# Expert outputs of a mixture-of-experts layer: gate weights applied at eviction, and rows added straight into the stored output by serial accumulating scatters

## What is computed

```python
x = x + _L0_ffn_ref(_layernorm(x, axis=-1), wg1, bg1, wg2, bg2, We, be)

h = gelu(xf @ wg1 + bg1, approximate=False)
logits = (h @ wg2 + bg2)[:, :E]                      # E = 20
probs = softmax(logits, axis=-1)
top_vals, top_idx = top_k(probs, K)                  # K = 2
gates = zeros((N, E)).at[arange(N)[:, None], top_idx].set(top_vals)
def body(y, eb):
    We_e, be_e, g_e = eb
    return (y + g_e[:, None] * (xf @ We_e + be_e), None)
```

## Time and profile before

| | |
|---|---|
| median of three runs | 693.65 us |
| the profiled execution | 695.27 us |
| its span, first to last instruction | 693.4 us |
| PE busy | 640.8 us, 92% |
| DVE busy | 443.1 us, 64% |
| ACT busy | 325.6 us, 47% |
| POOL busy | 295.4 us, 43% |
| mean granted TensorE clock | 0.961 of full speed |

### The profile page before, as it was taken

The page is one execution under the profiler, slowest core; times in us unless marked ns, Lnnn a source line. Parts: engine busy times, 40 slices in busy tenths (PEclk is TensorE's granted clock), DMA queues, the critical chain, the costliest instruction groups (busy, mean ns, idle before and its releaser), DMA issues. The chain is left out here.

```text
span 693.4 us, 15963 instructions
## 1 busy us (share of the span) xinstructions
PE 640.8 (92%) x6313; PEld 524.8 (76%) x6313; DVE 443.1 (64%) x1005; ACT 325.6 (47%) x604; POOL 295.4 (43%) x261
## 2 busy tenths in 40 slices
PE   5999999999999999999999979999999856999970
PEld 5668788887888878888788868887788735888850
DVE  4864656666656465575664557444577584999966
ACT  4344444544444344453443235334465422999930
POOL 2205544355434454435543235311244406788520
PEclk9999999999999999999999999999999956999995
DMA  8512465544665436654457530210011855999828
GB/s 329 196 48 50 122 171 124 148 115 125 170 169 119 124 99 170 149 121 125 124 117 182 121 132 16 77 62 2 3 62 62 305 212 193 403 402 360 292 91 323
DMA packets 42967, 107.75 MB, mean 155 GB/s; under 512 B 8180, under 2 KB 8564, under 8 KB 42114
## 3 DMA queue, kind: packets, MB, share of 16 engines
q1 hardware_dynamic: 38482, 98.21, 47.7%
q0 software_dynamic: 4400, 8.41, 3.3%
HBM read 65.61 MB, written 13.44 MB: 114 GB/s over the span
## 5 line engine op out<-in xcount | busy, mean ns | idle before, releaser
L1764 POOL TENSOR_SCALAR pp<-pp,rl 128x400 f32<-128x400 f32 x128 | 164.1, 1300 | 187.9 <-DVE rl L1240 187.8
L865 ACT ACTIVATE pp<-pp,acc 128x400 f32<-128x400 f32 x128 | 79.0, 620 | 66.5 <-DVE acc L1299 66.5
L1299 DVE CUSTOM_DVE_ANT_0 pp<-bank,cap 128x400 f32<-128x400 f32 x128 | 65.9, 571 | 50.9 <-PE bank L362 50.9
L192 PE MATMUL bank<-chi,wk 128*128 128x400 f32 x248 | 87.2, 351 | 0.0
L193 PE MATMUL bank<-clo,wk 128*128 128x400 f32 x248 | 85.5, 345 | 0.0
L194 PE MATMUL bank<-chi,wk 128*128 128x400 f32 x248 | 85.5, 345 | 0.0
L1291 DVE STREAM_TRANSPOSE raw<-pp 128x512 f32<-128x512 f32 x128 | 83.4, 688 | 2.2 <-POOL pp L1764 2.2
L192 PE MATMUL bank<-wv,chi 128*128 128x512 f32 x200 | 82.6, 413 | 0.0
L193 PE MATMUL bank<-wv,chi 128*128 128x512 f32 x200 | 79.3, 396 | 0.0
L194 PE MATMUL bank<-wv,clo 128*128 128x512 f32 x200 | 78.9, 395 | 0.0
L192 PE MATMUL bank<-wh,xu 128*128 128x512 f32 x148 | 62.1, 420 | 0.2 <-DVE xu L1148 0.2
(11 more groups left out here) (252 smaller groups left out, 1304.6 us busy)
## 6 DMA issues: line engine op xcount, KB each, us to landing
pt<-raw SPq DMA_DIRECT2D x256, 128.0 KB, 2.4
wr<-in_We SPq DMA_DIRECT2D x13, 1024.0 KB
craw<-in_ctx SPq DMA_DIRECT2D x15, 800.0 KB, 4.6
raw<-in_We SPq DMA_DIRECT2D x8, 1024.0 KB
acc<-in_We SPq DMA_DIRECT2D x6, 1024.0 KB
scratch_xn<-acc SPq DMA_DIRECT2D x16, 256.0 KB
wr<-scratch_ys SPq DMA_DIRECT2D x8, 512.0 KB, 7.5
x_sb<-in_x SPq DMA_DIRECT2D x2, 1024.0 KB, 12.0
```

The source lines that it names most:

```text
L192: pe.matmul(o, lhs[0], rhs[0], start=start, stop=False)
L865: act.activation(frame(p8), frame(p8), ACT.Exp, bias=bias, scale=-1.0, accum_out=total).then_inc(S["a_exp"], 1)
L1299: dve.tensor_tensor_reduce(out=frame(p8), in0=scores[:, p8 % 4, :], in1=cap[:, :], scale=-1.0, scalar=nm[:, b, p8:p8 + 1] if seg else 3e38 ...
L1764: pool.tensor_scalar(frame(p8), frame(p8), rl[:, n % 2, p8:p8 + 1], None, ALU.mult).then_inc(S["g_pn"], 1)
```

## The change

The gate is applied when a block is evicted, and the evicted rows are added into the output in DRAM.

1. The stream with the biases is stored to the output before the blocks. All eight bias products now stand before the blocks, and SP stores `x_sb` in two DMAs of 1 MB.
2. A table of gates `gtab` (row of the block by block) is made like `tab`: `row_in` times the one-hot of the block scaled by the gate. ScalarE scales (32 instructions), TensorE multiplies (16 matmuls), VectorE adds the high and low parts.
3. The eviction of block n is an activation with the scale `gtab[:, n]`, instead of a plain copy.
4. The scatter of block n goes to the output with `compute_op=ALU.add`. Two experts' blocks can hold the same token, so scatter n waits until scatter n - 1 has landed, and scatter 0 until both stores have.
5. The loading back, the 16 gate-weighted adds and the eight stores at the end are gone; so is `scratch_ys`. With the destination row being the token itself, the normalised rows are stored once, and a second index table `tok2` has the scatter's rows. An empty row 0 of a block is added, with gate 0, to some real row.

```diff
@@ TensorE, before the blocks
+            biases([3])
+            for j in range(16):
+                pe.wait_ge(S["a_gp"], j // 8 + 1)
+                last = pe.matmul(pb[7][:, 0:72], row_in[:, j, :], gate_in[:, j, :], start=(j == 0), stop=(j == 15))
+            last.then_inc(S["p_tab"], 1)
+            biases(range(4, 8))
             turn_tokens(0)
...
-            biases(range(3, 8))
@@ ScalarE, before the blocks
+            act.wait_ge(S["v_gw"], 1)
+            gates = [ghi[:, :, :].bitcast(f32), glo[:, :, :]]
+            for c in range(2):
+                act.wait_ge(S["v_tab"], c + 1)
+                for i in range(8):
+                    for part in range(2):
+                        ins = act.activation(gate_in[:, 8 * c + i, 36 * part:36 * part + BLOCKS], blk_in[:, 8 * c + i, :],
+                                             ACT.Copy, scale=gates[part][:, c, i:i + 1])
+                ins.then_inc(S["a_gp"], 1)
@@ ScalarE, in a block
                 if n >= 4:
                     act.wait_ge(d_yo[n % 4], 16 * (n // 4))
-                copy(yo[n % 4], pb[3 + n % 2][:, :]).then_inc(S["a_y"], 1)
+                elif n == 0:
+                    act.wait_ge(S["v_tok"], 2)
+                act.activation(yo[n % 4], pb[3 + n % 2][:, :], ACT.Copy, scale=gtab[:, n:n + 1]).then_inc(S["a_y"], 1)
@@ VectorE, routing
-            own.on(dve.tensor_tensor(gmg[:, :, :], gmg[:, :, :], sg[:, :].unsqueeze(1).to_broadcast([128, 2, 8]), ALU.mult))
+            chain(dve.tensor_tensor(gmg[:, :, :], gmg[:, :, :], sg[:, :].unsqueeze(1).to_broadcast([128, 2, 8]), ALU.mult))
+            chain(dve.tensor_copy(ghi[:, :, :], gmg[:, :, :]))
+            rest(glo[:, :, :], gmg[:, :, :], ghi[:, :, :]).then_inc(S["v_gw"], 1)
...
+            for i in range(8):
+                dve.wait_ge(S["p_be"], i + 1)
+                dve.tensor_tensor(x_sb[:, i, :], x_sb[:, i, :], pb[(0, 1, 2, 4)[i % 4]][:, :], ALU.add).then_inc(S["v_y"], 1)
+            dve.wait_ge(S["p_tab"], 2)
+            chain(dve.tensor_copy(gtab[:, :], pb[7][:, 0:BLOCKS]))
+            dve.tensor_tensor(gtab[:, :], gtab[:, :], pb[7][:, 36:36 + BLOCKS], ALU.add).then_inc(S["v_tok"], 1)
@@ VectorE, the end
-            biases(range(8))
-            for i in range(8):
-                dve.wait_ge(d_ga[i], 16)
-                for c in range(2):
-                    if c:
-                        dve.wait_ge(S["v_out"], 2 * i + 1)
-                    dve.scalar_tensor_tensor(out=x_sb[:, i, :], in0=yga[:, i, c, :], scalar=gmg[:, c, i:i + 1],
-                                             in1=x_sb[:, i, :], op0=ALU.mult, op1=ALU.add).then_inc(S["v_out"], 1)
@@ POOL, in a block
                 pool.wait_ge(S["a_y"], n + 1)
-                pool.indirect_dma_start(out=t["ys"][:, :],
-                                        out_offset=bass.IndirectOffsetOnAxis(ap=tok[:, n:n + 1], axis=0),
-                                        in_=yo[n % 4], in_offset=None, bounds_check=2 * T + BLOCKS - 1,
-                                        oob_is_err=False).then_inc(d_yo[n % 4], 16)
+                if n:
+                    pool.wait_ge(d_yo[(n - 1) % 4], 16 * ((n - 1) // 4 + 1))
+                else:
+                    pool.wait_ge(S["d_out"], 32)
+                pool.indirect_dma_start(out=out.rearrange("b q d -> (b q) d"),
+                                        out_offset=bass.IndirectOffsetOnAxis(ap=tok2[:, n:n + 1], axis=0),
+                                        in_=yo[n % 4], in_offset=None, bounds_check=T - 1, oob_is_err=False,
+                                        compute_op=ALU.add).then_inc(d_yo[n % 4], 16)
@@ SP, before the blocks
-            for n in (R, 6, 7, R + 1, R + 2):
+            load_weight(R)
+            ov = out.rearrange("(i b) q d -> (b q) i d", b=2)
+            for i in (0, 4):
+                sp.wait_ge(S["v_y"], i + 4)
+                sp.dma_start(ov[:, i:i + 4], x_sb[:, i:i + 4, :]).then_inc(S["d_out"], 16)
+            for n in (6, 7, R + 1, R + 2):
                 load_weight(n)
@@ SP, the end
-            for i in range(8):
-                sp.dma_start(yga[:, i], t["ys"][0:2 * T, :].rearrange("(c i p) n -> i p c n", c=2, i=8)[i]).then_inc(
-                    d_ga[i], 16)
-            for i in range(8):
-                sp.wait_ge(S["v_out"], 2 * i + 2)
-                sp.dma_start(out.rearrange("(i b) q d -> i (b q) d", b=2)[i], x_sb[:, i, :]).then_inc(S["d_out"], 16)
-            sp.wait_ge(S["d_out"], 128)
```

More of the change, by code:

```diff
@@ L130, in perceiver @@
         gmg = sb("gmg", [128, 2, 8])
+        ghi = sb("ghi", [128, 2, 8], f32r)
+        glo = sb("glo", [128, 2, 8])
+        gtab = sb("gtab", [128, BLOCKS])
         warm = sb("warm", [128, 1])
@@ L133, in perceiver @@
         tab = sb("tab", [128, BLOCKS])
-        tok = sb("tok", [128, BLOCKS], u32)
+        tok, tok2 = [sb(f"tok{j}", [128, BLOCKS], u32) for j in range(2)]
         m12 = sb("m12", [128, 2, 8, E])
@@ L148, in perceiver @@
         ji = sb("ji", [1, 16], i32)
-        cs2 = sb("cs2", [128, 576])
+        cs2 = sb("cs2", [128, 612])
         wr = sb("wr", [128, 4, 4, D])
@@ L156, in perceiver @@
         yo = [xm[:, 0, :], xm[:, 1, :], hT[:, 0:D], hT[:, D:T]]
-        yga = wr[:, 0:4].rearrange("p r (a c) n -> p (r a) c n", c=2)
         xflat = [v[:, :, :].rearrange("p k n -> p (k n)") for v in xu]
         row_in = xflat[1][:, 2048:4096].rearrange("p (j r) -> p j r", j=16)
+        gate_in = xflat[1][:, 0:16 * 72].rearrange("p (j b) -> p j b", j=16)
         put_in = [v.rearrange("p k n -> p (k n)")[:, 0:8 * 36].rearrange("p (j b) -> p j b", j=8) for v in g1]
@@ L168, in perceiver @@
         place1, iota, b128 = cs2[:, 360:376], cs2[:, 376:504], cs2[:, 504:504 + BLOCKS]
-        no_place = cs2[:, 539:539 + BLOCKS]
+        no_place, elsewhere = cs2[:, 539:539 + BLOCKS], cs2[:, 574:574 + BLOCKS]
         names = """d_cst d_k1 d_x0 d_x1 d_ctx d_cap d_xn d_raw0 d_raw1 d_par
@@ L177, in perceiver @@
             d_g1 d_gate a_g1 v_g1 p_g1 a_gelu p_lg v_lg a_le v_pre p_cnt v_orep v_tab p_tab v_tok v_ji
-            g_gt v_sg p_gT a_gT p_be v_y g_xi a_we v_we a_wx v_wx p_xo a_xo v_xo p_y a_y v_out d_out
+            g_gt v_sg p_gT a_gT p_be v_y g_xi a_we v_we a_wx v_wx p_xo a_xo v_xo p_y a_y v_gw a_gp d_out
             """.split()
@@ L183, in perceiver @@
         d_yo = [sem(f"d_yo{i}") for i in range(4)]
-        d_ga = [sem(f"d_ga{i}") for i in range(8)]
         d_x = (S["d_x0"], S["d_x1"])
@@ L699, in biases @@
                 for i in which:
-                    if i >= 3:
-                        pe.wait_ge(S["v_y"], i - 2)
+                    if i >= 4:
+                        pe.wait_ge(S["v_y"], i - 3)
                     r = slice(32 * (i % 4), 32 * (i % 4) + E)
-                    pe.matmul(pb[i % 3][:, :], gT[r, i // 4, :], be[r, :], start=True, stop=True).then_inc(S["p_be"], 1)
+                    pe.matmul(pb[(0, 1, 2, 4)[i % 4]][:, :], gT[r, i // 4, :], be[r, :], start=True, stop=True).then_inc(S["p_be"], 1)
             pe.wait_ge(S["g_gt"], 2)
@@ L1658, in vector @@
             chain(dve.tensor_tensor(rb[:, 1, :], slot, rb[:, 0, :], ALU.subtract))
-            dve.wait_ge(S["d_xn"], 272)
+            dve.wait_ge(S["d_xn"], 144)
             for c in range(2):
@@ L1681, in vector @@
             dve.tensor_copy(tok[:, :], tab[:, :]).then_inc(S["v_tok"], 1)
[L1683 to L1686, removed]
+            dve.wait_ge(S["v_tok"], 1)
+            chain(dve.scalar_tensor_tensor(out=tab[:, :], in0=tab[:, :], scalar=float(T), in1=elsewhere, op0=ALU.is_ge,
+                                           op1=ALU.mult))
+            chain(dve.scalar_tensor_tensor(out=tab[:, :], in0=pb[3][:, 0:BLOCKS], scalar=-1.0, in1=tab[:, :],
+                                           op0=ALU.add, op1=ALU.add))
+            own.on(dve.tensor_copy(tok2[:, :], tab[:, :]))
+            for i in range(8):
[4 more added lines that the diff above has]
+            dve.tensor_tensor(gtab[:, :], gtab[:, :], pb[7][:, 36:36 + BLOCKS], ALU.add).then_inc(S["v_tok"], 1)
             def turn_tokens(n):
@@ L1849, in load_tokens @@
                                         in_offset=bass.IndirectOffsetOnAxis(ap=tok[:, n:n + 1], axis=0),
-                                        bounds_check=2 * T + BLOCKS - 1, oob_is_err=False).then_inc(d_xi[n % X], 16)
+                                        bounds_check=T + BLOCKS - 1, oob_is_err=False).then_inc(d_xi[n % X], 16)
             def block_of(n):
@@ L1859, in block_of @@
                 pool.wait_ge(S["a_y"], n + 1)
[L1860 to L1863 removed]
+                if n:
[6 more added lines that the diff above has]
+                                        compute_op=ALU.add).then_inc(d_yo[n % 4], 16)
             pool.wait_ge(S["g_xi"], 1)
[L1866 removed]
+            pool.wait_ge(S["d_xn"], 144)
             pool.wait_ge(S["v_tok"], 1)
@@ L2006, in store_rows @@
                 sp.wait_ge(S["a_nx"], 8 + i + 1)
-                for c in range(2):
```

(17 more changed lines are left out.)

## The result

The changed kernel takes 762.83 us (761.92 to 764.02, four runs) against 693.48 us before: 1.099 times as long, 95% interval 1.097 to 1.1011. Forecast were 730.5 us in a range of 692 to 780. The direction and the mechanism were right. The size was not: 35 us slower were forecast, 69 came.

What follows compares the result with a forecast made beforehand. Bound before: TensorE at 3.19 us a block, POOL and DMA engines about as full. Start 0.5 us, blocks 54.0 and last landing 1.8 more, less 21.0 for the tail: 35.3 us slower, 730.5 us, range 692 to 780.

Steps and rivals of the forecast that it cites:

- the mechanism: Expert blocks: each adding scatter waits for the previous landing; first to last scatter takes 132.8 us instead of 78.8.
- the tail's saving: After the last scatter's landing: reading back, gate-weighted adds and stores go, giving back 21.0 us.
- where the crowd ends: Expert blocks: last weight asked for about scatter 13, so 14 periods at 5.8 us, then 12 at 4.3 us.
- P = L + 0.3: Expert blocks: period from scatter to scatter, or 3.19 us if that is more; 5.8 us crowded, 4.3 us quiet.
- L: Adding scatter, start of issue to landing: 4.0 us quiet, up to 7.9 us in a crowd.
- 2.8 + (2.22 - 0.98): Quiet adding scatter: quickest gather, then the last plain scatter's time without its issue, in series: 4.0 us.
- the end: After the blocks: output complete when the last adding scatter lands, 4.0 us after its issue, at 728.6 us of span.
- the start: Ahead of the blocks: first scatter 0.5 us later, at 591.8 us; VectorE's first tokens 1.8 us later, covered by POOL's gathers.
- rival A: Expert blocks: add hidden, landing under 2.9 us, TensorE keeps 3.19 us a block, tail gone; 676.6 us, chance 0.11.
- B: Rival, expert blocks: mild crowding, quiet 3.5 us landing throughout, period 3.8 us; 696 us, no change, chance 0.08.
- C: Rival, expert blocks: always crowded or add itself slow, landings 6.7 to 7.9 us; 782 to 815 us, chance 0.07.
- D: Rival, expert blocks: TensorE falls to 1.2 GHz, 6.3 us a block; 762 us, chance 0.06 in full.

Runs made afterwards that it cites:

- the free plain version: Changed kernel with plain scatters into four tensors in turn, each waiting only for the fourth before it, full weights: 684.24 us.
- two chains: Changed kernel with even blocks added into the output, odd ones into a second tensor, each scatter waiting for the one before the last: 701.68 us.

## Why the prediction was right or wrong

**Right: the mechanism.** One landing after another sets the pace, and the tail's saving does not pay for it. With four adding scatters in flight instead of one, 66 us are saved (762.8 against 696.9).

**Right: where the crowd ends.** The last weight was asked for at 681.23 us, with scatter 13 issued at 682.00. The two kinds of period are there, 6.94 and 5.57 us, though both are longer than the 5 to 6 and 4 to 4.5 us that were to show it.

**Wrong: P = L + 0.3.** This is the term that was mis-sized first. The 0.3 us were read between instructions of POOL with nothing to wait for. One that has waited is issued 0.84 to 0.87 us after the landing, and the trace of before showed it. Its last eviction:

```profile
668.78 0.61 ACT hT L799
```

The last scatter's issue began at 670.15 us, 0.76 us after that eviction ended. Over 26 periods the difference is 0.54 x 26 = 14 us.

**Wrong: L.** The mean landing was 5.5 us (6.31 a period, less 0.84), not 4.8: another 0.67 x 26 = 17 us. Quiet it is 4.8 and not 4.0: 1.55 us of issue and a flight of 3.2. The sum 2.8 + (2.22 - 0.98) took its write from the last plain scatter, which carried an almost empty block (0.01 MB above); the other quiet plain ones landed after 2.6 us. And an adding scatter takes 0.57 us longer to issue. These two more than cover the 0.8 us. For crowded periods I had 5.5 us, and they showed 6.1, with 7.7 and 8.7 for the first two.

**Wrong: the end.** The time from the last landing to the end was put at nothing. The last scatter landed after 3.6 us, 0.4 sooner than the 4.0 in the sum, but POOL's DRAIN kept the execution open, and 2.7 us went by before the end of the span.

14 + 17 us for the periods and 2.7 for the end, less 0.4 for the last landing and 0.7 for the earlier first scatter, make up the 33 us between the forecast span of 728.6 and the 761.5 us measured.

**Right by luck: the start.** The first scatter was issued at 591.11 us, forecast were 591.8. But the blocks' own start moved more than I said. From the gate product to VectorE's first token step it took 16.5 us before (564.13 to 580.62) and now 20.8:

```profile
562.45 0.17 DVE L1659 TENSOR_TENSOR gmg<-gmg,sg 128x16 f32<-128x16 f32 x1
...
574.26 3.63 PE L720 MATMUL bank<-xu 128*128 128x72 f32 x16
577.82 2.09 PE L705 MATMUL bank<-be,gT 20*128 20x512 f32 x8
579.93 2.48 DVE L1710 TENSOR_TENSOR x_sb<-x_sb,bank 128x512 f32<-128x512 f32 x4 [3.87 <-PE bank L705]
583.22 1.29 DVE L1166 TENSOR_TENSOR xu<-bank,xu 128x512 fp32r<-128x512 f32 x2 [0.47 <-issue]
...
589.55 0.69 ACT L1147 ACTIVATE xm<-bank,gtab 128x512 f32<-128x512 f32 x1 [7.10 <-PE bank L196]
```

That is 4.3 us more and not 1.8. VectorE waited 3.9 us for the last four bias products, which TensorE, at 1.2 GHz, had only begun 2.1 us before. POOL's gathers did not cover it, as the sum had them do. POOL was through with them at 589.6 us; the eviction of block 0 began at 589.55, 3.6 us later than before, and took 0.69 us where I had kept 0.6. The first scatter waited for it and was 1.2 us later than it could have been. The time came out right because routing stood 1.7 us earlier in this execution (the gate product at 562.45 against 564.13 us), which was not forecast and which no run here explains. The two stores had landed by 588.6 us and held nothing up, as forecast.

In the free plain version the late start is one part of why it took 684 and not the 676.6 us of rival A. Late weights are another (ScalarE waited 2.7 us for them, and TensorE was busy 56.4 of 58 us). The end is a third: A counted 2.8 us from the issue of the last scatter, and there it was 5.8, POOL's DRAIN again.

**Rivals.** A needed L under 2.9 us. In the chain even a plain scatter kept it only while the engines were quiet (2.6 us), and from 620 to 680 us its median was 4.7. B fell with the quiet 4.8. C did not come: the spacing shrank behind the last load. D's 762 us lie next to the measured time by luck: the granted clock was 0.82 to 0.94 in the stretches above, and TensorE was held up by POOL, not POOL by TensorE. ScalarE waited 73.5 us in all for output buffers to come free (39.5 and 34.0).

The rule of "DMA: Bandwidth & Descriptors" in the Trainium skill (2.0 us and the bytes over 436 GB/s), by which A would have come, fits the quiet plain landing of 2.2 to 2.6 us. It does not fit the adding one of 4.8, not even with the bytes counted twice (2.7 us by the estimate in the prediction).

## What to carry to other kernels

A chain of dependent DMAs costs issue, flight and wake-up for every link; read the wake-up from an instruction that really waited, and compare the whole link with the period of the loop before trading a tail for it. What a DMA adds in work was nearly free here while several were in flight and the engines had room (1.4 us for all adds), and appeared as late loads once they were full (12.6 us). Look for what can be in flight together first: two chains won back 61 of 69 us, before the cost of joining them. And do not take a cost from the last instance of a loop before looking at what it carried.

## What the runs showed of the hardware that was not expected

- POOL issues an indirect DMA 0.3 us behind the instruction before it, but 0.8 us after an event for which it had to wait, be it ScalarE (0.76 and 0.87) or a landing (0.84 to 0.87).
- An adding indirect scatter of the same rows takes 1.55 instead of 0.98 us to issue, lands after 4.8 instead of 2.6 us when quiet, and has 64 packets more; halving the rows' bytes brings it to 3.7 us.
- POOL's DRAIN at the end of the program lasts 5.6 us from the issue of the last plain scatter and 6.2 us from that of the last adding one. Where that scatter is the last work, the execution goes on for 2.7 us after it has landed.
